# Attention value products spread over all score steps instead of two of every three

## The reference

```python
ct_q = x @ Wd_q_w + Wd_q_b
query = heads(ct_q @ Wu_q_w + Wu_q_b) + heads(_rope(ct_q @ Wq_r_w + Wq_r_b, cos, sin))
ct_kv = x @ Wd_kv_w + Wd_kv_b
key = heads(ct_kv @ Wu_k_w + Wu_k_b) + heads(_rope(x @ Wk_r_w + Wk_r_b, cos, sin))
value = heads(ct_kv @ Wu_v_w + Wu_v_b)
attn = jax.nn.softmax(jnp.einsum('bhqd,bhkd->bhqk', query, key) / scale, axis=-1)
out = jnp.einsum('bhqk,bhkd->bhqd', attn, value)        # then @ Wo_w + Wo_b
x = _layernorm(x + out)                                 # 4096 x 256
x = _layernorm(x + ffn(x))    # x rounded to int8 by one scale, times int8 weights
```

## Time and profile before

| | |
|---|---|
| median of three executions | 1985.05 us (1983.85 to 1987.11) |
| profiled execution | 1983.67 us |
| its span, first to last instruction | 1981.9 us |
| ScalarE (ACT) busy | 1815.3 us, 92% of the span |
| TensorE (PE) busy | 1851.2 us, 93% |
| VectorE (DVE) busy | 1582.6 us, 80% |
| granted TensorE clock, mean | 0.982 |
| exponentials at L800: first and last start | 157.6 and 1888.7 us |

### The profile page before, as it was taken

The page is one execution under the profiler, slowest core; times in us unless marked ns, Lnnn a source line. Parts: engine busy times, 40 slices in busy tenths (PEclk is TensorE's granted clock), DMA queues, the critical chain, the costliest instruction groups (busy, mean ns, idle before and its releaser), DMA issues.

```text
span 1981.9 us, 31796 instructions
## 1 busy us (share of the span) xinstructions
PE 1851.2 (93%) x13009; PEld 451.9 (23%) x13009; DVE 1582.6 (80%) x1500; ACT 1815.3 (92%) x2026; POOL 163.4 (8%) x134
## 2 busy tenths in 40 slices
PE   8967999999999999999999999999999999999955
PEld 3441112122121221221222222222122122222134
DVE  3653888888888888888888887888988898888458
ACT  4447999999999999999999999999999999999935
POOL 5723500000000000000000000000000300000012
PEclk9998999999999999999999999999999999999987
DMA  5644111101111111111121000111111101101012
GB/s 165 216 161 174 25 25 25 25 20 19 21 20 22 25 25 25 25 25 25 25 67 25 17 17 17 25 25 25 25 25 25 23 19 19 21 18 24 1 44 85
DMA packets 165483, 81.48 MB, mean 41 GB/s; under 512 B 130204, under 2 KB 146716, under 8 KB 164856
## 3 DMA queue, kind: packets, MB, share of 16 engines
q1 hardware_dynamic: 164024, 78.11, 15.3%
q10 hardware_dynamic: 1312, 1.32, 0.2%
HBM read 48.83 MB, written 29.23 MB: 39 GB/s over the span
## 4 chain that ended last, share of the span: by engine, by line
ACT 69%; PE 10%; issue 9%; DVE 6%; DMA 2%; POOL 2%; SPq 1%; ACTq 0%; DVEq 0%; POOLq 0%
ACT arena L800 55%; ACT parts_or_sums L800 14%; PE PS L601 5%; PE PS L558 3%; PE PS L640 1%; DVE arena L860 1%; PE PS L1044 1%; POOL arena L1363 1%; DVE bn L728 1%; DMA Qst<-parts_or_sums 1%; DMA arena<-arena 1%; POOL arena L1362 1%; DVE arena L1654 1%; POOL arena L1365 0%; DMA arena<-head_out 0%
## 5 line engine op out<-in xcount | busy, mean ns | idle before, releaser
L800 ACT ACTIVATE arena<-PS 128x1024 f32<-128x1024 f32 x1488 | 1396.5, 1134 | 31.4 <-PE PS L558 31.0
L601 PE MATMUL PS<-arena,Vh 128*32 128x512 f32 x6704 | 1082.6, 606 | 5.5 <-DVE arena L860 3.6
L558 PE MATMUL PS<-Qst,Kst 49*128 49x512 f16 x4096 | 710.7, 384 | 61.4 <-ACT arena L800 38.2
L860 DVE SCALAR_TENSOR_TENSOR arena<-arena 128x2048 f32<-128x2048 f32 x282 | 646.4, 2292 | 0.1
L836 DVE TENSOR_SCALAR arena<-PS 128x512 int32<-128x512 f32 x376 | 259.6, 690 | 269.4 <-PE PS L558 265.5
L558 PEld LDWEIGHTS PS<-Qst,Kst 49*128 49x128 f16 x4096 | 182.3, 93 | 1048.9 <-ACT arena L800 797.6
L601 PE MATMUL PS<-parts_or_sums,Vh 128*32 128x512 f32 x1488 | 386.0, 604 | 0.0
L800 ACT ACTIVATE parts_or_sums<-PS 128x1024 f32<-128x1024 f32 x372 | 369.3, 1137 | 2.8 <-PE PS L558 2.8
L601 PEld LDWEIGHTS PS<-arena,Vh 128*32 128x32 f32 x6704 | 155.9, 108 | 278.6 <-issue 270.0
L856 DVE SCALAR_TENSOR_TENSOR arena<-arena 128x2048 f32<-128x2048 f32 x94 | 216.0, 2297 | 0.0
L844 DVE TENSOR_SCALAR arena<-arena 128x2048 int32<-128x2048 int32 x94 | 115.7, 1230 | 7.3
(11 more groups left out here) (115 smaller groups left out, 606.6 us busy)
## 6 DMA issues: line engine op xcount, KB each, us to landing
Kst<-k_halves SPq DMA_DIRECT2D x64, 128.0 KB
Qst<-q_halves SPq DMA_DIRECT2D x64, 128.0 KB
Vh<-head_values SPq DMA_DIRECT2D x30, 256.0 KB, 4.4
arena<-xT_dram SPq DMA_DIRECT2D x8, 512.0 KB, 5.2
k_halves<-parts_or_sums SPq DMA_DIRECT2D x16, 256.0 KB, 2.4
k_whole<-arena SPq DMA_DIRECT2D x8, 512.0 KB, 3.3
q_halves<-parts_or_sums SPq DMA_DIRECT2D x16, 256.0 KB, 3.2
q_whole<-arena SPq DMA_DIRECT2D x8, 512.0 KB, 4.4
```

What stands on the lines that cost most here:

```text
L558: return nc.tensor.matmul(out, Kst[par][low:low + HK + 1, at:at + 128], Qst[par][low:low + HK + 1, j * CH:(j + 1) * CH], start=True, stop= ...
L601: last = nc.tensor.matmul(bank(value_bank(t))[32 * j:32 * j + 32, :], Vh[t % 2][:, kt, :], moving, start=kt == first, stop=kt == last_kt)
L800: nc.scalar.activation(ring(at, k), bank(g % SLOTS * SLOT, k), ACT.Exp, scale=EXP_SCALE).then_inc(a.exp, 1)
L860: last = nc.vector.scalar_tensor_tensor(out=t, in0=t, scalar=POLY[3 - j], in1=power if j == 3 else mantissa, op0=ALU.add, op1=ALU.mult)
```

## The change

One number is added to the table of phases: value products may stand in any step.

```diff
 LAG = 4
-VALUE_PHASES = (0, 1)
+VALUE_PHASES = (0, 1, 2)
 BLOCK_PHASES = (2, 1)
```

## The result

The changed kernel took 1979.61 us (median of 10 runs, 1975.48 to 1981.68) against 1984.91 us for the kernel before. The ratio is 0.9968, with a 95% interval of 0.9959 to 0.9978: 0.3% faster, about a fifth of the gain that was forecast (1958 us, with a range of 1950 to 1971). The profiled execution took 1976.98 us, 6.7 us less than the one of before.

What follows compares the result with a forecast made beforehand. TensorE's lateness was taken to hold up ScalarE's exponentials. Gains of 21.4 - 2 + 7.1 + 0.5 = 27.0 us gave 1956.7 us profiled, 1958 us as a median; range 1950 to 1971 us.

Steps and rivals of the forecast that it cites:

- ScalarE's own pace, 0.903 us: In the attention, ScalarE by itself was taken to need 0.903 us per exponential, read between starts of records.
- the 52.4 us called excess: Attention time in which ScalarE was kept from starting: 1731.1 us measured less 1678.7 us at 0.903 us each.
- Ordinary heads, 21.4 less 2 us: 26.8 heads go from 0.87 to 0.07 us of waiting each: 21.4 us, less 2 us for waits on VectorE.
- The lateness that was worked out at the end of head 8: In the old order TensorE's lateness reaches 1.42 us against 1.12, so ScalarE waits 0.3; in the new 1.05, no wait.
- The room, 1.12 us: How late TensorE may reach the scores of step s+3 after exponential s before ScalarE waits; bounded between 1.0 and 1.18.
- the rule: Carries TensorE's lateness from step to step, never below 0; ScalarE waits for whatever passes the room.
- Projections, 7.1 us: In the five heads holding fifteen of the sixteen projections, waiting falls from 19.7 to 12.6 us.
- The first head and VectorE's late places, 0.5 us: First head and two places where VectorE is late: long waits stay, some catching up behind them goes, 0.5 us.
- VectorE's closer blocks, 0: 41 gaps of three steps instead of 11 make VectorE 0.27 us late after each: cost 0, or 8 us without cover.
- The last stage, unchanged: The stage after the attention was to keep its 92 us.
- ScalarE's own pace is the bound: Rival: small unnamed delays in the attention are ScalarE's own; gain 0 to 14 us, about 1978 us; chance 0.06.
- The estimate of 0.946 us: Spacing of 1024-column ACTIVATEs by the skill's rule, above the mean of 0.931; then nothing could be gained: 1985 us.

Runs made afterwards that it cites:

- ScalarE alone: No layer computed and TensorE idle: 160 exponentials of 128x1024, then 160 of 128x512; the 1024-column ones end 0.9166 us apart and start 0.904 apart.
- w1 to w3: Changed kernel plus filling matmuls in the last stage: 20 of 49 rows (1975.40 us), fp32 in three places (1984.25 us), six fp32 in the first place alone (1973.39 us).
- the version faster than both: Changed kernel plus six fp32 filling matmuls before the last projection, and VectorE's six weight-splitting operations spread behind six blocks: 1971.15 us, ratio 0.9928 to the kernel before.

## Why the prediction was wrong, step by step

- **ScalarE's own pace, 0.903 us.** This step failed, and with it the sum. The pace is 0.9165 us: shown by ScalarE alone (0.9166 between ends), and by the ordinary heads of the changed kernel, of w1 to w3 and of the version faster than both, which all take 53.17 us for 58. Of the 52.4 us called excess, 1859 x 0.0135 = 25 us are ScalarE's own work.
- **Ordinary heads, 21.4 less 2 us.** Measured 2.1. The term rested on the failed pace. The lateness that was worked out at the end of head 8 was real, and the late start of the earlier trace rows too, but between ends (642.57 and 645.41, from the groups of ScalarE around it) the three exponentials took 2.84 us where 2.75 are the least: 0.09 us lost, not 0.3.
- **The room, 1.12 us.** It was fitted so that the rule gave the 0.87 us a head of the false excess, and the fit also gave 19.7 us for the projections' heads exactly as measured. Two agreements came from one error: both numbers held the same 0.8 us a head. A room of 1.25, with the right pace, forecast the two runs with extra matmuls.
- **Projections, 7.1 us.** Right in kind; measured 5.2, by the rule with the right pace 5.8.
- **The first head and VectorE's late places, 0.5 us.** Heads 4, 22 and 26 gave 3.3 us and head 0 took 0.6 more. Of the 3.3 us, 2.5 are a clock that held at two waits where it fell in the run with these heads in the new order: luck, and no forecast.
- **VectorE's closer blocks, 0.** Right: TensorE waited for L836 1.5 us against 1.3.
- **The last stage, unchanged.** Wrong by 3.3 us in the profiled execution. No instruction there changed, but behind a wait that both kernels have the granted clock was 1.2 GHz for 13.7 us in place of 6.8, so that five groups of L640 ran slow and not two. The forecast gave no reason for its nothing but that the change touches the attention alone; why the slow stretch was longer stays open.
- **The rivals.** "ScalarE's own pace is the bound" had 0.06 and a time of about 1978; it is what happened, and the time came out at 1979.6. That the times are so near is in part luck, since the last stage's loss and the clock at two waits were in neither. I held against it that an unnamed delay stood where TensorE was late. It did, and cost nearly nothing: at the end of head 8 the starts ran 0.3 us late, and the ends 0.09. The estimate of 0.946 us from the Trainium skill ("ScalarE: Activation LUTs", section "What ACT_TABLE_LOAD costs") that I set beside it is not borne out, since 0.9166 was measured. But the conclusion drawn from it, that the starts have little to give, was nearer than mine.

## What to carry to other kernels

Read ScalarE's pace between the ends of records, and test it in a stretch where the record lengths stay level; where records grow longer from one to the next, the starts run ahead, and a gap between starts is no loss. A constant fitted until a rule reproduces the trace proves nothing about a second constant that was assumed: the check must be a row that the fit did not use. A change that evens out an engine's work buys room, and is worth only the places that lacked it.

## What the runs showed of the hardware

- Records of back-to-back ACTIVATEs on 128x1024 begin every 0.904 us and end every 0.9166; the lead grew to a record length of 3.0 us after 160 of them, and on 512 columns stopped at 3.89.
- TensorE with a quarter of the passes for the value products was granted 1.2 GHz for 942 and 526 us on end, with its records still covering 99% of the time: less work came with a lower clock, and the kernel took 1985.57 us, as long as before the change.
- Behind a wait of 4.7 us TensorE ran slow for about two groups of L640 in one execution and for about five in another. Six fp32 matmuls on all rows (5.4 us) kept it at 2.4 GHz; 20 fp16 ones on 49 rows (4.5 us, and 0.7 us idle behind them) did not.
